# Indirect stores and gathers of an expert layer: each issue on GpSimd waits for the landing of the second to last

## The reference

```python
x = layernorm(x + attention(x))          # 16 heads, causal
scores = sigmoid(x @ gate_w)
_, selected = top_k(scores + expert_bias, 2)
top_scores = scores[selected] / sum(scores[selected])
shared = silu(x @ shared_gate_w) * (x @ shared_up_w) @ shared_down_w
routed = 0
for e in range(16):
    g, u = split(x @ experts_gate_up[e])         # 256 -> 2 x 128
    routed += comb[:, e] * (silu(g) * u @ experts_down[e])    # 128 -> 256
out = layernorm(x + shared + routed)
```

## Time and profile before

| what | value |
|---|---|
| median of three runs | 985.3 us |
| the three runs | 978.0, 985.3, 985.47 us |
| span of the profiled execution | 975.7 us |
| TensorE busy | 854.0 us (88%) |
| VectorE busy | 660.1 us (68%) |
| ScalarE busy | 476.2 us (49%) |
| GpSimd busy | 300.0 us (31%) |
| indirect stores | 64, mean 988 ns of GpSimd each |
| indirect gathers | 64, mean 974 ns of GpSimd each |

### The profile page before, as it was taken

The page is one execution under the profiler, slowest core; times in us unless marked ns, Lnnn a source line. Parts: engine busy times, 40 slices in busy tenths (PEclk is TensorE's granted clock), DMA queues, the critical chain, the costliest instruction groups (busy, mean ns, idle before and its releaser), DMA issues. The chain is left out here.

```text
span 975.7 us, 18404 instructions
## 1 busy us (share of the span) xinstructions
PE 854.0 (88%) x5476; PEld 478.9 (49%) x5477; DVE 660.1 (68%) x1527; ACT 476.2 (49%) x686; POOL 300.0 (31%) x368
## 2 busy tenths in 40 slices
PE   7979799999999989999999997799898999999300
PEld 4635434444444434444444432687556777777200
DVE  6428688888888887888888870489892122466364
ACT  3423266656666656656666566455322444444100
POOL 3423312211112111221112211442477500464373
PEclk9979899999999999999999999889899999999755
DMA  8773855444764266425754000710126745766443
GB/s 285 193 205 131 162 67 75 100 97 59 131 85 89 36 117 118 68 38 106 130 66 57 9 2 25 235 65 23 60 103 210 232 137 152 207 207 211 157 126 95
DMA packets 82464, 113.95 MB, mean 117 GB/s; under 512 B 8945, under 2 KB 60401, under 8 KB 82417
## 3 DMA queue, kind: packets, MB, share of 16 engines
q1 hardware_dynamic: 57808, 78.01, 38.1%
q0 software_dynamic: 6720, 18.88, 5.9%
q10 hardware_dynamic: 17888, 16.41, 5.2%
HBM read 62.55 MB, written 50.33 MB: 116 GB/s over the span
## 5 line engine op out<-in xcount | busy, mean ns | idle before, releaser
L658 ACT ACTIVATE work<-ps 128x1024 f32<-128x1024 f32 (+3 forms) x384 | 293.8, 811 | 185.5 <-PE ps L725 185.3
L335 DVE TENSOR_REDUCE m_neg<-ps 128x1 f32<-128x512 f32 (+3 forms) x432 | 265.6, 662 | 29.2 <-PE ps L320 18.7
L629 POOL TENSOR_SCALAR_AFFINE_SELECT work<-work 128x512 f32<-128x512 f32 x128 | 81.2, 634 | 394.4 <-ACT work L658 390.0
L317 PE MATMUL ps<-stacks 96*128 96x512 bf16 (+3 forms) x528 | 151.9, 332 | 1.5 <-DVE m_neg L335 1.5
L725 PE MATMUL ps<-stacks 99*128 99x512 bf16 (+3 forms) x528 | 124.6, 329 | 6.4 <-PEq L371 4.8
L335 DVE TENSOR_REDUCE m_neg_late<-ps 128x1 f32<-128x384 f32 (+3 forms) x176 | 106.7, 636 | 27.4 <-PE ps L320 27.4
L740 PE MATMUL ps<-work,vg 128*32 128x512 f32 (+3 forms) x1056 | 112.5, 498 | 1.6 <-POOL work L629 1.6
L320 PE MATMUL ps<-mask_b,ident_b 128*128 128x128 bf16 x512 | 100.3, 223 | 0.0
L317 PEld LDWEIGHTS ps<-stacks 96*128 96x128 bf16 x528 | 50.0, 98 | 95.0 <-DVE m_neg L335 48.8
L1243 DVE TENSOR_TENSOR work<-work,ps 128x256 f32<-128x256 f32 x48 | 20.2, 421 | 106.7 <-ACT work L1062 106.7
L1421 PE MATMUL ps<-wgu,work 128*128 x384 | 91.7, 382 | 0.3 <-issue 0.3
(11 more groups left out here) (143 smaller groups left out, 1098.4 us busy)
## 6 DMA issues: line engine op xcount, KB each, us to landing
stacks<-qk_parts SPq DMA_DIRECT2D x132, 128.0 KB, 6.3
qk_parts<-work SPq DMA_DIRECT2D x32, 384.0 KB, 3.0
y_sorted<-work SPq DMA_DIRECT2D x8, 1536.0 KB, 9.9
work<-y_sorted SPq DMA_DIRECT2D x48, 256.0 KB
z_sorted<-work ACTq DMA_DIRECT2D x48, 256.0 KB
wgu<-qk_parts SPq DMA_DIRECT2D x60, 128.0 KB, 6.5
work<-in_xT SPq DMA_DIRECT2D x8, 512.0 KB, 4.8
work<-in_x SPq DMA_DIRECT2D x8, 512.0 KB, 3.6
```

Source lines behind the costliest of these rows:

```text
L317: mm = pe.matmul(dst, qs[r][0:KS, h0 + m, qt * P:(qt + 1) * P], ks[r][0:KS, h0 + m, half * CH:half * CH + w], start=True, stop=not diag)
L335: dve.tensor_reduce(dst, ps[:, bank, 0:heads * w].rearrange("p (h k) -> p h k", h=heads), AX.X, ALU.max, negate=True).then_inc(reduced, 1)
L629: pool.affine_select(out=blk_, in_=blk_, compare_op=ALU.is_ge, fill=0.0, base=0, pattern=[[0, GH], [1, P]], channel_multiplier=-1).then_in ...
L658: act.activation(probs[:, s + 2 * pair:s + 2 * pair + 2, off:CH], ps[:, SCORE_BANK + 2 * pair:SCORE_BANK + 2 * pair + 2, off:CH], ACT.Exp, ...
```

## The change

The stores of pick 0 and pick 1 get semaphores of their own, and each store waits until the store before it with the same pick has landed. In the gathers, the second of a tile (j = 1) waits until both gathers of the tile before have landed. SyncE now waits for two semaphores of a section where it waited for one.

```diff
-            scattered = [sem(f"scattered{g}") for g in range(SECTIONS)]
+            scattered = [[sem(f"scattered{g}{j}") for j in range(TOPK)] for g in range(SECTIONS)]
...
-                    sp.wait_ge(scattered[g], 16 * TOPK * SEC_TILES)
+                    for j in range(TOPK):
+                        sp.wait_ge(scattered[g][j], 16 * SEC_TILES)
...
                 def scatter(t):
                     g = t // SEC_TILES
                     for j in range(TOPK):
+                        wait_count(pool, scattered[g][j], 16 * (t - g * SEC_TILES))
                         pool.indirect_dma_start(
                             out=y_sorted[g], out_offset=bass.IndirectOffsetOnAxis(ap=row_of[:, j, t:t + 1], axis=0),
-                            in_=y_all[:, t, :], in_offset=None).then_inc(scattered[g], 16)
+                            in_=y_all[:, t, :], in_offset=None).then_inc(scattered[g][j], 16)
 
                 def gather(u):
                     wait_count(pool, both_added, u - ZSLOTS + 1)
                     for j in range(TOPK):
+                        if j == 1 and u > 0:
+                            pool.wait_ge(gathered[(u - 1) % ZSLOTS], 16 * TOPK * ((u - 1) // ZSLOTS + 1))
                         pool.indirect_dma_start(
                             out=zg[u % ZSLOTS][:, j, :], out_offset=None, in_=z_sorted[u // SEC_TILES],
                             in_offset=bass.IndirectOffsetOnAxis(ap=row_of[:, j, u:u + 1], axis=0))\
```

## The result

The changed kernel takes 993.36 us in the median of four runs (989.36 to 994.48), the kernel before 981.65 in its four (974.74 to 985.47). The ratio is 1.0115, with a 95% interval of 1.0059 to 1.0172. That is 11.7 us more, on the chip of this comparison. On two other chips, used for experiments further down, the changed kernel with one of its stores moved forward took over 4% less than the kernel before, and that is the larger finding of this study.

A forecast was written before the change was run, and what follows sets the result against it. It took the chain to run through GpSimd's issue of indirect DMAs twice (section 0's stores, section 1's gathers), with TensorE's experts between. Terms 3.5 + 3 + 7.5 = 14 us on 985.3 gave 999.3 us, range 987 to 1011.

The forecast's parts named there:

- What decides the change: At each waiting indirect DMA: landing plus the way to the next start (0.05 to 0.31 us) against GpSimd's two steps, 2.53.
- Stores of section 0: Ahead of the experts, on the path: pairs take 2.71 us in place of 2.53, plus late landings; 3.5 us, ends 0 and 9.
- Stores of section 1: Right after section 0's stores: some 3 to 9 us longer, but done before their rows are wanted; 0 us.
- Gathers of section 0: Beside the experts: the first chunk's store, queued behind gather 13, goes out later and holds VectorE; 3 us, ends 0 and 11.
- Gathers of section 1: Behind the experts, on the path: 12 tiles take 3.04 us in place of 2.51, plus late landings; 7.5 us.
- Waits nearly free: Rival: GpSimd prepares the next DMA while waiting and gathers land in 2.7 us even beside the experts; 990 us, chance 0.22.
- the gathers become the bound: Rival, experts' stage: section 0's gather landings stay at 4.0 to 4.4 us, that term is 9 to 12; 1007 us, chance 0.20.
- the change does nothing: Rival: landings under 2.2 us with the way included, so the time stays at 985.3 us; chance 0.05.
- Faster: Rival: with two under way gathers land in 2.4 us, late landings go and the experts win 2 us; 982 us, chance 0.05.

The follow-up runs named there:

- e6: Changed kernel, but each store waits for the landing of the last one and the gathers don't wait; 1076.07 us in a single run.
- e1: Changed kernel without the waits in the gathers, so only the stores of both sections wait; 981.98 us, ratio 1.0018 to the kernel before.
- e2: Changed kernel with only the gathers of section 0 waiting, stores and section 1's gathers free; 982.34 us, ratio 1.0018 to the kernel before.
- e3: Changed kernel with only the gathers of section 1 waiting, stores and section 0's gathers free; 987.94 us, ratio 1.0081 to the kernel before.
- e9: Kernel before, without added waits, with the first chunk's store moved ahead of gather 12; 1040.79 us on chip C, ratio 0.9964.
- r8: Changed kernel with the first chunk's store moved ahead of gather 12, same kernel as e8; 998.81 us on chip C, ratio 0.9578 to the kernel before.
- e8: Changed kernel with the first chunk's store moved ahead of gather 12; 995.73 us on chip B, ratio 0.9563 to the kernel before.

## Why the prediction was right or wrong

The predicted 999.3 us stood on a median of 985.3; on that footing the measured 11.7 us make 997.0. Measured are 993.36, inside 987 to 1011, and slower by over 1% was the likeliest.

*What decides the change* held. The way from a landing to the next start was put at 0.31, with 0.05 as its other end; it is 0.27. That this preparation is not hidden by the wait was the one reading on which the sign rested for the stores, and it is shown by the steps of 2.69 (changed) and 2.68 (e6).

*Stores of section 0*: 3.5 taken, 2.74 measured, and 2.6 in e1. The pairs gave 15.5 x 0.16 = 2.5, late landings some 0.5 where I had added 1.6, and the last store landed 0.3 us sooner than in the trace of before. *Stores of section 1* at nothing: in e1 the stretch beside the experts is no longer than before.

*Gathers of section 0*: 3 taken, 2.17 measured, and 3.5 in e2. The mechanism was the forecast one, but in other parts: against the start of the stage the store went out 1.3 us later (890.76 - 2.51 = 888.25, for 886.95) where I had 3.2, and it landed in 5.0 us in place of 3.4, which I had not foreseen. Together VectorE's instruction came 2.9 us late (893.29 for 890.42), and the two errors nearly cancel.

*Gathers of section 1*: 7.5 taken, 7.55 measured from the first gather to the last landing (921.09 to 972.56 + 3.10 = 975.66, 54.57 us, against 47.02). e3 alone gives it again. That it fits to 0.1 is partly luck: a waiting tile took 3.09 in place of 3.04 us, which gives 7.0 for the 12, and late landings some 0.5, where I had 6.4 and 1.9 and had then gone down to 7.5.

*Waits nearly free* fell by the 0.27; *the gathers become the bound* fell as landings had a median of 3.4 beside the experts, where 3.8 was before; *the change does nothing* fell by the three stretches.

*Faster* was wrongly built, and this is the step that failed, though not on the chip of the comparison. I had bounded a relief of the other engines by TensorE's busy share beside indirect DMAs, at 2 us, and on the first chips none shows. On chip C the relief is 42 us (e9 1040.79, r8 998.81), and on B e8 is 48 under before. Nothing in the rows of before could show it, since that execution has no such wait at all; I took one chip's trace as the kernel's nature. The change itself, with the store in its old place, was not run there; e9 and r8 differ by its waits alone, so for the change itself the finding needs only that the store's place, worth some 3 us on A, does not undo it.

## What to carry to other kernels

A wait for the second to last costs landing plus way (here 2.42 or 2.8, and 0.27) less the two steps that the engine takes anyway (2.5), times the pairs on the path; with two of these numbers within 10% of each other, read them to a hundredth and per place. Look at what else is queued behind the waiting engine: the store of a finished chunk cost beside the experts what the gathers did not. And measure a limit on DMAs under way on more than one chip before dropping it: here two under way cost 1.2% where engines were undisturbed and, with the store moved, won over 4% where they were not, while a limit of three cost 0 to 1.2 us in its stretches and protected from little or nothing (ratios 0.991 and 0.9963). Taking work off the engine that sets the pace shortens its stretch, but look at the end as well: 4.4 us won in the gathers left about one.

## What the runs showed of the hardware that was not expected

- Two chips of those used ran the kernel before in 1043.9 and 1043.5 us where another had 979.5, run after run (23, 25 and 24 runs), and their traces have stalls of ScalarE, VectorE and TensorE of up to 30 us beside indirect DMAs of GpSimd, with the DMA engines 0.27 to 0.30 busy (e9). The kernel before itself has no trace from there; e9 differs from it by the place of one store. With two under way 57.8 us of such waits on the chain become 19.1 (r8) or none (e8's fastest run).
- In such a stall the semaphores that matmuls raise go up to 24 us after the matmul's modelled end (e9), 0.01 us in an undisturbed execution, and no packet of an instruction queue moves in the two longest.
- The landing of an indirect store of 128 rows of 1 KB is 2.4 us whether the one before it has landed (e6) or not; that of a gather is 2.7 to 2.8 with nothing else going on.
- A gather that had to wait takes GpSimd 1.07 us in place of 0.95, and lands 0.1 later, at the end of the changed kernel; beside the experts it keeps 0.95 there.
- The store of 512 KB behind the gathers landed in 5.0 and 5.4 us with the waits, in 3.4 and 3.3 without.
